# Two scatters of the slot table issued ahead of the base sum in the steps of the first attention

## The reference

```python
x = x + xattn(layernorm(x), ctx, ctx)            # 16 heads of 16, softmax over 361 context rows, then Wo, bo
xf = layernorm(x).reshape(-1, 256)               # 1600 rows
xn = xf / max(norm(xf), 1e-12)                   # the length of each normalised row
group_scores, expert_scores = xn @ gc.T, xn @ ec.T + bias
# the 4 best of 8 groups, of their experts the 4 best: top_idx; gates = softmax(top_scores)
pos = cumsum(onehot(top_idx))                    # place of each choice in its expert's list of 250
keep = pos < 250
buf[e, pos] = xf[token]                          # rows for the experts
x = x + shared(xf) + sum over the 4 choices of gate * expert(buf)
```

## Time and profile before

| what | us |
|---|---|
| median of 3 runs | 1676.21 |
| lowest and highest of them | 1673.42, 1678.94 |
| the profiled execution, its own time | 1666.83 |
| its span in the profile | 1664.7 |
| PE busy | 1487.7 |
| DVE busy | 790.6 |
| POOL busy | 479.4 |

### The profile page before, as it was taken

One profiled execution on the slowest core, in us unless ns is written; L12 is line 12 of the kernel. 1 busy time (PEld: TensorE's weight loads), 2 busy tenths in 40 slices (PEclk: granted clock), 3 DMA queues, 4 the chain that ended last, 5 costly groups with the idle time before them and its releaser, 6 DMA issues. The chain is left out here.

```text
span 1664.7 us, 30297 instructions
## 1 busy us (share of the span) xinstructions
PE 1487.7 (89%) x11672; PEld 1119.9 (67%) x11672; DVE 790.6 (47%) x2238; ACT 701.7 (42%) x1473; POOL 479.4 (29%) x428
## 2 busy tenths in 40 slices
PE   6999997998888999999999957898799999939996
PEld 3666664666665668888888824565466667629885
DVE  6577574567765422222222246765566666541111
ACT  3464464666666112222222234456656555502221
POOL 2122122011334536666666420111111111012332
PEclk9999997999999999999999977999899999959998
DMA  7343556697772217777777527357477776339995
GB/s 300 121 146 97 159 163 111 122 171 125 127 132 60 61 40 196 201 199 194 196 195 195 137 48 168 85 111 148 93 143 128 122 134 120 67 110 328 325 297 151
DMA packets 252439, 250.86 MB, mean 151 GB/s; under 512 B 116724, under 2 KB 226700, under 8 KB 246796
## 3 DMA queue, kind: packets, MB, share of 16 engines
q1 hardware_dynamic: 210316, 221.13, 52.7%
q0 software_dynamic: 41984, 27.84, 9.9%
HBM read 194.10 MB, written 54.58 MB: 149 GB/s over the span
## 5 line engine op out<-in xcount | busy, mean ns | idle before, releaser
L2831 PE MATMUL cross_ps_score<-cross_q,cross_k 128*128 128x250 f32 x1024 | 223.5, 376 | 0.8 <-DVE cross_q L3312 0.8
L2831 PEld LDWEIGHTS cross_ps_score<-cross_q,cross_k 128*128 128x128 f32 x1024 | 195.5, 191 | 23.9 <-DVE cross_q L3312 1.0
L3321 DVE TENSOR_TENSOR cross_prob<-cross_act_,cross_ps_score 128x250 f32<-128x250 f32 x128 | 53.2, 416 | 268.3 <-ACT cross_act_ L2999 268.3
L3412 POOL DMA_INDIRECT x_sum<-cross_ye,cross_token x64 | 128.6, 2009 | 80.9 <-ACT cross_ye L3005 68.7
L1745 ACT ACTIVATE layer_parts<-layer_ps_prob 128x400 f32<-128x400 f32 (+1 forms) x192 | 97.0, 508 | 106.4 <-PE layer_ps_prob L1561 103.9
L3026 DVE TENSOR_REDUCE cross_nmax<-cross_ps_score 100x2 f32<-100x722 f32 x128 | 112.1, 903 | 61.8 <-PE cross_ps_score L2579 61.5
L2861 ACT ACTIVATE cross_prob<-cross_ps_prob 128x400 f32<-128x400 f32 (+1 forms) x192 | 96.3, 508 | 87.6 <-PE cross_ps_prob L2612 86.8
L2999 ACT ACTIVATE cross_act_<-cross_ps_score 128x250 f32<-128x250 f32 x128 | 48.6, 380 | 167.6 <-PE cross_ps_score L2831 167.6
L2843 PE MATMUL cross_ps_prob<-cross_val,cross_prob 128*125 128x256 f32 x512 | 115.8, 379 | 0.0
L3587 ACT ACTIVATE experts_h<-experts_ps_h,experts_b 128x128 f32<-128x128 f32 x160 | 45.7, 368 | 138.8 <-PE experts_ps_h L3556 138.8
L3402 POOL DMA_INDIRECT cross_xe<-ln_rows,cross_token x64 | 79.6, 1244 | 81.7 <-PE cross_ps_misc L2817 57.5
(11 more groups left out here) (471 smaller groups left out, 3111.1 us busy)
## 6 DMA issues: line engine op xcount, KB each, us to landing
packed_sb<-in_w SPq DMA_DIRECT2D x20, 1024.0 KB, 7.0
experts_w<-in_w SPq DMA_DIRECT2D x20, 1024.0 KB
k_stack<-mixer_part SPq DMA_DIRECT2D x32, 541.5 KB, 3.9
cross_k<-in_wg SPq DMA_DIRECT2D x32, 512.0 KB, 5.4
cross_k<-in_wu SPq DMA_DIRECT2D x32, 512.0 KB, 6.9
cross_val<-in_wd SPq DMA_DIRECT2D x32, 512.0 KB, 5.2
layer_stacks<-k_stack SPq DMA_DIRECT2D x30, 270.8 KB, 5.3
cross_k<-k_stack SPq DMA_DIRECT2D x25, 270.8 KB
```

Of the source, the lines that this page charges most:

```text
L2831: ins = nc.tensor.matmul(ps_pre[m][:, side, 0:CAP], w[s][:, k, m * P:(m + 1) * P], xt[s][:, k, :], start=(k == 0), stop=(k == KD - 1))
L3321: nc.vector.tensor_tensor(up[s][:, m, :], act_[:, m % 2, :], ps_pre[m][:, 1, 0:CAP], ALU.mult).then_inc(v_gated[m][s], 1)
L3412: g.indirect_dma_start(prog.x_sum, bass.IndirectOffsetOnAxis(token[:, 2 * e + t:2 * e + t + 1], 0), ye[s][:, t, :], None, compute_op=ALU.a ...
```

## The change

On POOL, in the steps b = 8 to 14, `set_base(b + 1)` and the first two scatters change places. The wait for `zeroed`, which stands ahead of the very first scatter, moves with them. No instruction is added or removed, and the programs of PE, DVE, ACT and SP are the same in both.

```diff
                 for b in range(B):
-                    if b + 1 < B:
-                        set_base(b + 1)
                     if b == 2 * G:
                         g.wait_ge(zeroed, 16)
                     if b >= 2 * G:
                         scatter(b // G - 2, b % G * TOPK, TOPK // 2)
+                    if b + 1 < B:
+                        set_base(b + 1)
                     if b > 0:
                         root(b - 1)
                         inverse_length(b - 1)
```

## The result

| | before | after |
|---|---|---|
| median, us | 1675.4 (6 runs, 1668.4 to 1682.81) | 1691.48 (6 runs, 1686.41 to 1703.56) |
| the profiled execution, us | 1666.83 | 1690.11 |
| its span, us | 1664.7 | 1688.1 |

The ratio is 1.011, with a 95% interval of 1.0081 to 1.0139. The changed kernel is 16 us slower, and the forecast was 3.7 us faster.

The account below looks back on a forecast made before the run. PE was taken as nearest to the bound, waiting on a chain ending at POOL. Seven distances of 31.81 us against 28.14 gave 3.67 us; 1676.2 - 3.7 = 1672.5 us, range 1667.5 to 1678.0.

Parts of the forecast that it names:

- The root waits for `var` alone: POOL, steps 8 to 14: without scatters ahead of the root, `xf` starts 0.89 us behind `var` instead of 2.23.
- third `values` to `logits`: Distance on PE in steps 8 to 14, forecast to fall to the 4.02 us of steps without scatters.
- 3.67 us: Excess of the seven distances on PE in steps 8 to 14, 31.81 against 28.14 us, forecast to come back.
- The forecast 3.7 us: Whole kernel: gain from the early root in steps 8 to 14, median 1672.5 us; chance 0.70.
- two scatters issued in that part of the step (those behind `inverse_length`) cost PE nothing: Step part from `logits` to the next third `values`: scatters there were claimed to add 0 to PE's time.
- 12.48 = 12.48: From `logits` to the next third `values`, a step without scatters and a held one both take 12.48 us.
- 9.4 us below the median of the three runs: Profiled execution of before, 1666.83 us against 1676.21; the 3.7 us were simply taken from the median.
- The rival on the slower side: Steps 8 to 14: DVE stands still for each of 14 moved scatters, 10.2 us more, 1686.4 us; chance 0.04.
- Base sum: hidden: POOL, steps 8 to 14: the base sum's 0.73 us hides under DVE's statistics and costs nothing.
- Loads: Rival: scatters delay transfers of keys and queries, 1 us in each of seven steps, 1679.5 us; chance 0.03.

Follow-up runs that it names:

- group 3: Follow-up runs on one chip without holds: plain DMAs, four scatters in mid step, one then three scatters, and the kernel before at 1665.73 us.
- e4: Against the kernel before: no scatters inside the loop, the first two groups' 32 moved behind it, early root; ratio 1.0184 to before, loop 92.25 us.
- group 1: Follow-up runs on one chip that held, testing four other orders of scatters and root; the kernel before took 1674.45 us there.
- f1: Changed kernel with each of the 64 indirect scatters replaced by a plain DMA from POOL; profiled once, not timed; loop 97.33 us.

## Why the prediction was wrong

- The root waits for `var` alone, `xf` 0.89 us behind it, third `values` to `logits` in 4.02 us: right in all seven steps. On the chip of group 3, where nothing holds, the early root (with one and three scatters) gave a loop of 92.23 us against 94.88 and 0.996 (0.9942 to 0.9977) of before; the six distances inside the loop account for 26.75 - 24.12 = 2.63 of 3.67 us, and the loop gained 2.65. The forecast 3.7 us are 0.998, so the gain there was at least what was forecast. The changed kernel itself never ran on that chip; that it gains there is argued, not shown.
- The step that failed: "two scatters issued in that part of the step (those behind `inverse_length`) cost PE nothing", and from it that each step keeps its length when two more follow them. The row behind it (12.48 = 12.48) was read for a pair and used for a run of four. With four in a row the loop took 117 to 122 us where 92.3 were due, 25 to 29 us more, in each of the four profiled executions of the changed kernel.
- The row was also taken from an execution without holds. The prediction noted that it lay 9.4 us below the median of the three runs and only moved the sum by that; it did not ask what those runs had that the profile had not. The second profile of before shows it: 5.4 us more in the loop, 4.7 of them between third `values` and `logits`. The third one, on the chip that does not hold, has the first one's 94.88 us again. So the first looks like one from a chip without holds, though which chip it ran on is not known.
- The rival on the slower side had the right cause, the moved scatters, and nearly the size (1686.4 us), but another mechanism: DVE standing still for them. Beside the scatters of step 10 DVE's two maxima from 443.86 take 1.73 us, and 1.72 from 449.14 without one; it is PE's signals that stood still. These maxima read one operand from PSUM. But the two-input operations of DVE on SBUF did not stand still either: the 39 that lie beside a scatter in the four profiles of the changed kernel, from 280 to 600 us, took at most 56 ns more than without one (`cross_hot` 747 ns at the most, 691 to 693 without).
- Base sum: hidden, as said; POOL still idles 7.09 us ahead of it. Loads: no wait of PE for keys in the loop; that rival did not come about.
- The price is not in proportion to the run: 0.4 to 0.6 us of loop for pairs at the early place, 8.5 with three in a row, 25 to 30 with four. I read it so, without a run that tests it by itself: a short hold lies in the slack of ACT and DVE; a longer one makes PE idle, and then the clock halves: `project` (L2652, 4 matmuls) took 1.99 us in the changed kernel's step 10, and 1.07 at full clock in the kernel before.

A run of scatters is not enough for a hold. Right behind the loop the same execution of the changed kernel has six in a row, from 559.01 to 566.55, beside a busy PE (timeline, PE's `to_rows` and DVE's answer as in step 10 above):

```profile
560.39 1.00 POOL L3361 DMA_INDIRECT row_token<-cross_choice,cross_row_put  x1 [0.30 <-issue]
561.08 0.60 PE L2638 MATMUL cross_ps_misc<-packed_sb,cross_acc 128*100 128x128 f32 x4
561.69 0.99 POOL L3361 DMA_INDIRECT row_token<-cross_choice,cross_row_put  x1 [0.30 <-issue]
561.72 0.26 DVE L3042 RECIPROCAL cross_rden<-cross_ps_misc 100x16 f32<-100x16 f32 x1 [4.52 <-PE cross_ps_misc L2638]
562.98 0.99 POOL L3361 DMA_INDIRECT row_token<-cross_choice,cross_row_put  x1 [0.30 <-issue]
```

DVE starts 0.04 us behind PE, where in step 10 it started 2.77 us behind. In the other three profiles of the changed kernel the same signal is 0.02 us late at the most there, and e4, on the chip of group 1, shows none late in its 36 until PE runs out of work at 546.58. Further behind there are late ones again: one of the changed kernel's, due at 585.03 beside eight scatters in a row, comes at 586.87, and e4's, due at 591.33 and 594.01 beside another eight, come at 600.24 and 600.34. So neither the number in a row nor PE's being busy decides alone; what else does was not tested.

What stays open is the cause of the hold: by what path PE's signals are late while POOL issues indirect DMAs in the steps of the loop, what else of a step it takes, and what differs between the chips. The Trainium skill, page DMA: Bandwidth & Descriptors, section "SWDGE vs HWDGE vs iDMA", says that GpSimd builds the descriptors of its plain and its indirect DMAs alike in software. The plain ones of f1 did not hold in their 2.3 us, in which indirect pairs held a little; that speaks against this common part as the cause, but is no proof.

## What to carry to other kernels

Be wary of indirect DMAs on POOL that follow each other where PE and the other engines hand each other small pieces of work: in these steps four in a row cost 4 to 6 us each, while two, then 1.5 us without one, early in the step, were nearly free. It is no law: right behind the loop six in a row delayed nothing. So look for late signals in the trace before paying for a split. When moving an instruction, look at what it becomes the neighbour of, not only at the idle time that it fills. A profiled execution that lies well below the median of the plain runs is a warning that it lacks something that they have; profile again, on another chip if there is one.

## What the runs showed of the hardware

- Beside indirect scatters of 100 elements of 8 bytes on POOL, PE's signals to DVE, ACT and SP came up to 3.4 us late in the runs of four (5.0 us long) of the changed kernel, and were let go 0.8 to 1.0 us behind the end of most of them. (The expectations speak of 4.2 and 5.8 us; put against PE's instructions one by one, the signals do not bear these out.) DVE's, as far as the trace holds them, were not late. Behind the loop PE's were on time in a run of six and, in e4, up to 8.9 us late beside a run of eight.
- It depends on the chip or its state in a call: of the five chips of the groups four held, with the kernel before at 1669.94 to 1674.45 us; one did not, at 1665.73 us. The same two files, run in mid step and three in a row, held on one and not on the other.
- PE idle for 2.55 us in step 10 of the changed kernel was followed by 3.4 us at a granted clock of 0.50; four of its matmuls (`project`) took 1.99 us there and 1.07 at 1.00.
- DVE's two-input operations on SBUF beside an indirect scatter took at most 56 ns more than alone (39 of them, four profiles).
